# Last 64 value channels of a window-attention block: five products become three, with one more VectorE transpose and a GpSimd sum

## What is computed

```python
xl = roll(layernorm(transpose(x)), (-3, -3))                  # tokens x 192 channels
xw = windows(xl, 7)                                           # 49 tokens in each window
q, k, v = split(einsum('bnc,oc->bno', xw, qkv_w) + qkv_b)     # 6 heads of 32 channels
attn = softmax(einsum('bhnd,bmhd->bhnm', q, k) * 32 ** -0.5)
out = einsum('bhnm,bmhd->bnhd', attn, v)
out = out @ proj_w.T + proj_b
xl = layernorm(roll(unwindow(out), (3, 3)))
h = gelu(xl @ fc1_w.T + fc1_b) @ fc2_w.T + fc2_b              # 192 -> 768 -> 192
return transpose(h) + x
```

## Time and profile before

| | us |
|---|---|
| median of 3 runs | 2952.38 (2946.92 to 2953.0) |
| the profiled execution, whole | 2930.57 |
| its span in the trace | 2928.8 |
| TensorE busy | 2876.8 (98% of the span) |
| ScalarE busy | 2686.3 (92%) |
| VectorE busy | 2612.4 (89%) |
| GpSimd busy | 1287.7 (44%) |

### The profile page before, as it was taken

How to read it: one execution, slowest core, us unless ns; L and a number is a source line. 1 busy time by engine, 2 the same in 40 slices (tenths; PEclk the granted TensorE clock), 3 DMA queues, 4 the chain that set the end, 5 groups by cost and what they waited for, 6 DMA issues and landing times.

```text
span 2928.8 us, 72487 instructions
## 1 busy us (share of the span) xinstructions
PE 2876.8 (98%) x25004; PEld 2787.5 (95%) x25004; DVE 2612.4 (89%) x7211; ACT 2686.3 (92%) x5500; POOL 1287.7 (44%) x1549
## 2 busy tenths in 40 slices
PE   5999999999999999999999999999999999999998
PEld 4899999999999999999999999999999999999998
DVE  7889999999999999998989898999989999899985
ACT  2899999999999999999999999999999999999996
POOL 3444444444444444444444444444444444444432
PEclk9999999999999999999999999999999999999999
DMA  5344444434443444343444434444443443444431
GB/s 112 81 97 90 89 90 89 99 86 93 95 89 86 94 99 86 85 100 85 92 93 89 97 84 94 95 89 91 92 96 86 94 97 86 94 88 96 87 80 34
DMA packets 675019, 263.32 MB, mean 90 GB/s; under 512 B 505699, under 2 KB 633444, under 8 KB 674660
## 3 DMA queue, kind: packets, MB, share of 16 engines
q1 hardware_dynamic: 670724, 257.00, 40.9%
q10 hardware_dynamic: 3936, 1.68, 0.3%
HBM read 169.23 MB, written 89.27 MB: 88 GB/s over the span
## 4 chain that ended last, share of the span: by engine, by line
PE 81%; SPq 14%; DVE 1%; issue 1%; POOL 1%; DMA 1%; ACT 0%; POOLq 0%; DVEq 0%; ACTq 0%
PE psum L331 8%; PE psum L334 7%; PE psum L332 7%; PE psum L333 7%; PE psum L335 7%; PE psum L623 6%; PE psum L597 5%; PE psum L577 4%; PE psum L578 4%; PE psum L588 4%; PE psum L589 4%; PE psum L579 4%; PE psum L603 4%; SPq L410 3%; SPq L467 3%; PE psum L598 2%
## 5 line engine op out<-in xcount | busy, mean ns | idle before, releaser
L1268 POOL TENSOR_TENSOR pr<-pr,rc 98x294 f32<-98x294 f32 x512 | 384.5, 760 | 371.0 <-DVE rc L1079 371.0
L778 ACT ACTIVATE hh<-psum,b 128x392 fp32r<-128x392 f32 x768 | 451.3, 588 | 32.7 <-PE psum L589 6.4
L781 ACT ACTIVATE hf<-psum,b 128x392 f32<-128x392 f32 x768 | 451.3, 588 | 6.4
L1043 DVE TENSOR_TENSOR hl<-hf,hh 128x392 fp32r<-128x392 f32 x640 | 373.8, 599 | 4.2 <-ACT hf L781 4.1
L1241 POOL TENSOR_TENSOR ve<-mv,eps 104x4 f32<-104x4 f32 (+1 forms) x256 | 81.7, 319 | 660.0 <-DVE mv L1003 660.0
L1066 DVE TENSOR_REDUCE mx<-psum 98x6 f32<-98x294 f32 x512 | 229.1, 447 | 113.8 <-PE psum L598 113.5
L1262 POOL TENSOR_TENSOR hl<-hf,hh 128x392 fp32r<-128x392 f32 x128 | 133.2, 1041 | 358.7 <-ACT hf L781 358.7
L577 PE MATMUL psum<-hh,w2h 128*128 128x392 f32 x768 | 272.4, 355 | 0.0
L735 ACT ACTIVATE pt<-psum 113x294 f32<-113x294 f32 x512 | 205.8, 402 | 68.8 <-PE psum L603 68.6
L597 PE MATMUL psum<-km,qm 128*98 128x98 f32 x2048 | 260.8, 249 | 7.9 <-DVE xn L1008 3.9
L331 PE MATMUL psum<-x_h,w_mh 128*128 128x392 f32 x768 | 265.0, 345 | 0.7 <-DVE pr L1071 0.7
(11 more groups left out here) (135 smaller groups left out, 9929.0 us busy)
## 6 DMA issues: line engine op xcount, KB each, us to landing
bc<-mean_rstd SPq DMA_DIRECT2D x128, 392.0 KB, 3.7
xg<-in_x SPq DMA_DIRECT2D x368, 96.0 KB, 2.4
values_by_token<-vt_m SPq DMA_DIRECT2D x128, 256.0 KB
vbd<-values_by_token SPq DMA_DIRECT2D x256, 96.0 KB
xt<-in_x SPq DMA_DIRECT2D x112, 194.5 KB, 2.8
out<-xt SPq DMA_DIRECT2D x112, 194.5 KB, 3.3
values_by_token<-vt_r SPq DMA_DIRECT2D x128, 128.0 KB
vbd<-values_by_token SPq DMA_DIRECT2D x256, 51.0 KB
```

What stands on the lines that cost most here:

```text
L778: nc.scalar.activation(hh[:, m % HB, :], bank("fc1", m)[:, 0:T], ACT.Gelu, bias=b1[:, m:m + 1]).then_inc(s_hh, 1)
L781: nc.scalar.activation(hf[:, m % HB, :], bank("fc1", m)[:, 0:T], ACT.Gelu, bias=b1[:, m:m + 1]).then_inc(s_gelu, 1)
L1268: nc.gpsimd.tensor_tensor(probs(j), probs(j), each, ALU.mult).then_inc(s_prob, 1)
```

## The change

The high and the low weights of the last 64 value channels are laid side by side as one stationary tile of 128 columns, `wv_m` for the first 128 input channels and `wv_r` for the last 64. One matmul then gives the product with the high weights in PSUM partitions 0 to 63 and that with the low weights in 64 to 127. `values_rest` takes three matmuls in place of five. VectorE transposes the lower partial result (partitions 64 to 127) with one more instruction into a new tile `vt_l` in partitions 0 to 63, and GpSimd adds `vt_l` to `vt_r`. SyncE's queue waits for that sum before it writes `vt_r` to DRAM.

```diff
@@ last_read
             if name == "vt":
-                return s_vt, v, 2, i
+                return s_vt, v, 3, i + 1
@@ values_to_dram
-                sp.wait_ge(s_vt, nth(u, 2, 1))
+                sp.wait_ge(s_vt, nth(u, 3, 2))
...
                 sp.dma_start(by_token[u % 2, 0:CM], vt_m[:, u % 2]).then_inc(s_vd, 16)
+                sp.wait_ge(s_vsum, nth(u, 1, 0))
                 sp.dma_start(by_token[u % 2, CM:C], vt_r[:, u % 2]).then_inc(s_vd, 16)
@@ values_rest
-                claim(u, [("vt", 0)], (s_lo["x1"], 2, 1))
-                five(bank("vt", 0)[0:CR, 0:T], wq, CM, CR, [p[:, :] for p in x1]).then_inc(s_pe["vt"], 1)
+                claim(u, [("vt", 0)], (s_lo["x1"], 2, 0))
+                ps = bank("vt", 0)[:, 0:T]
+                nc.tensor.matmul(ps, wv_m[:, :], x1[0][:, :], start=True, stop=False)
+                nc.tensor.matmul(ps, wv_m[:, :], x1[1][:, :], start=False, stop=False)
+                pe.wait_ge(s_lo["x1"], nth(u, 2, 1))
+                nc.tensor.matmul(ps, wv_r[:, :], x1[2][:, :], start=False, stop=True).then_inc(s_pe["vt"], 1)
@@ split (once, before the loop)
+                if n == 0:
+                    for pair, raw_, of in ((wv_m, sm_, w[0]), (wv_r, sr_, w[2])):
+                        nc.vector.tensor_copy(pair[:, 0:CR], of[:, CM:C].bitcast(F32))
+                        nc.vector.tensor_tensor(pair[:, CR:128], raw_[:, CM:C], of[:, CM:C].bitcast(F32), ALU.subtract)
@@ v_out
-                blocks = bass.AP(psum, BANK_OF["vt", c] * 512, [[8 * 512, (CR, CM)[c]], [N, NW], [N - DH, 2], [1, DH]])
-                nc.vector.transpose((vt_r, vt_m)[c][:, u % 2], blocks).then_inc(s_vt, 1)
+                def blocks(r0, m):
+                    return bass.AP(psum, r0 * 8 * 512 + BANK_OF["vt", c] * 512, [[8 * 512, m], [N, NW], [N - DH, 2], [1, DH]])
+
+                if c == 0:
+                    nc.vector.transpose(vt_r[:, u % 2], blocks(0, CR)).then_inc(s_vt, 1)
+                    if u > 0:
+
+                        dve.wait_ge(s_vsum, nth(u - 1, 1, 0))
+                    nc.vector.transpose(vt_l[:, :, :, :], blocks(CR, CR)).then_inc(s_vt, 1)
+                else:
+                    nc.vector.transpose(vt_m[:, u % 2], blocks(0, CM)).then_inc(s_vt, 1)
@@ gpsimd
+            def last_values(u):
+
+                pool.wait_ge(s_vt, nth(u, 3, 1))
+                nc.gpsimd.tensor_tensor(vt_r[:, u % 2], vt_r[:, u % 2], vt_l[:, :, :, :], ALU.add).then_inc(s_vsum, 1)
@@ gpsimd step, after times_rstd_rest
+                if u[2] is not None:
+                    last_values(u[2])
```

More of the change, by code:

```diff
@@ L136, in swin_block_program @@
         w1 = [sb(f"w1_{p}", [128, NF], F32R) for p in ("mh", "ml", "rh", "rl")]
+        wv_m = sb("wv_m", [128, 128], F32R)
+        wv_r = sb("wv_r", [128, 128], F32R)
         w2h = sb("w2h", [128, MT, C], F32R)
@@ L188, in swin_block_program @@
         vt_r = sb("vt_r", [CR, 2, NW, 2, DH])
+        vt_l = sb("vt_l", [CR, NW, 2, DH])
         by_token = nc.dram_tensor("values_by_token", [2, C, NW, 2, DH], F32)
@@ L242, in swin_block_program @@
         s_vt = sem("values_by_token")
+        s_vsum = sem("last_values_summed")
         s_vd = sem("values_in_dram")
```

## The result

The changed kernel takes 2979.47 us (median of 4 runs, 2975.81 to 2980.7), the kernel before 2950.23 us beside it; the ratio is 1.0102, 95% interval 1.0083 to 1.0121. It is slower by 1.0%, 29 us, where 23 us were forecast; its profiled execution took 2978.32 us. A second comparison, beside the experiments, gave 1.0130 (1.0114 to 1.0145). The kernel before took 2950 us in the first comparison and 2928 to 2931 us in the four rounds of the experiments, which ran on three chips; the chip of the first comparison is not known, so it is not shown that a chip makes this difference.

A forecast was written before the change was run, and what follows sets the result against it. The prediction took TensorE as the bound, busy 2746 of 2750 us. A longer step (20 us) plus GpSimd's sum (3 us) made 23 us slower, from 2952.38 to 2975 us (+0.8%), range 2946 to 2994.

The forecast's parts named there:

- The slack of 0.21 us at `project`: Time from the end of VectorE's `vt_m` to TensorE's weight load for `project` 0, taken as the deciding number.
- Two matmuls at 0.18 us each: TensorE in `values_rest`: two products fewer free 0.36 us a step, 45 us over 124 steps.
- so I take nothing for it: TensorE in `values_rest`: 128 output columns in place of 64 cost the remaining three products nothing.
- The transpose: VectorE ahead of `o_r`: one more transpose adds 0.63 to 0.71 us a step, 0.71 taken.
- Release and reload: TensorE at `project`: starts 0.06 or 0.14 us after `vt_m` ends, then loses 0.05 to 0.10 us reloading weights.
- I take the middle, 0.16: Growth of one step, stated as 0.05 to 0.26 us; over 124 steps, middle 20 us slower.
- the cheap transpose: VectorE's new transpose by plain overlap with its neighbour: 0.63 us in place of 0.71.
- The sum on GpSimd: Before `rstd`: about 1.4 us long, mostly covered by idle time; costs 0 to 8 us in all, 3 taken.
- SyncE's queue: Stores and loads behind the new wait for the sum: delay hidden or already priced, nothing taken.
- the work before the loop: Four small VectorE instructions building the paired weights, hidden by a 6.2 us DMA wait; nothing taken.
- Rival A: TensorE keeps its gain of 0.36 us a step: 45 us faster, 2907 us; chance 0.17.
- Rival C: GpSimd's sum contends with VectorE, grows to some 2.5 us, delays `xn` in half the steps: 3006 us; chance 0.06.

The follow-up runs named there:

- the late transpose: The changed kernel with VectorE's transpose of the lower partial result moved behind `vt_m`; ratio 1.0008 to the kernel before.
- three matmuls alone: The changed kernel without `vt_l`, its transpose and GpSimd's sum; ratio 0.9958 to the kernel before.
- late transpose and swap: The changed kernel with the lower transpose behind `vt_m` and ScalarE's `gelu_full` of tile 1 ahead of the first `k_rest_out`; ratio 0.9978 to the kernel before.

## Why the prediction was right

*The slack of 0.21 us at `project`* decided, as said: 124 waits there, none elsewhere of any size. Shown by the late transpose, which takes this wait away and leaves the work of every engine as it is. Of the 0.21 us the release itself takes 0.11; the prediction has it as a term of its own.

*Two matmuls at 0.18 us each.* Right as the price of two products more of the same kind (0.34 us a step with five against three). But the step "so I take nothing for it", on the 128 columns, left out the first weight load: the change frees 0.30 us of TensorE, not 0.36. It did not matter for the forecast, since I let VectorE use only 0.30; from the row maximum to `xt` it is now 8.15 us (1518.08 to 1526.23) against 8.43, so 0.28.

*The transpose.* Forecast 0.71 us in a range from 0.63. It took 0.72 us, and its follower starts 0.76 us after it started (1527.57 to 1528.33); from `xt` to the end of `vt_m` it is 3.72 us against 2.97, so 0.75. The new transpose and its follower each start only after the one before has ended (1527.55 to 1527.57, 1528.29 to 1528.33), as the rule that the prediction quotes from the Trainium skill (VectorE: DVE Perf Modes, section "Two Vector instructions with no wait between them") has it.

*Release and reload.* Forecast 0.06 to 0.14 and 0.05 to 0.10 us. Measured 0.11 from the end of `vt_m` to the load and 0.14 to the product; the second product of `project` then comes 0.14 us after the first (1530.09 to 1530.23), where it was 0.08 (1525.38 to 1525.46), so reloading costs 0.06. With these the step closes: from the start of the row maximum to the end of `vt_m` 11.87 us in place of 11.40, from there to `project` 0.14 in place of 0.39, and from `project` to the next row maximum 10.51 in place of 10.48, together 0.25.

*The term that was too small* is "I take the middle, 0.16" for the growth of the step: 0.26 was measured, the upper end of the stated 0.05 to 0.26. With 0.71 as chosen for the transpose the working gives 0.13 to 0.26; the middle that I took also weighed the cheap transpose, which I had already set aside. This is 12 us of the sum.

*The sum on GpSimd.* Forecast 1.4 us long, 0 to 8 us in price, 3 taken; 1.35 us long and about 7 us in price. The median needs no further term: 32 + 7 = 39 us is above the 29 us of the first comparison and beside the 38 us of the second (0.0130 x 2931). Why the two comparisons differ by 0.3% was not tried. That the 29 us lie so near to the forecast 23 is therefore in part luck: the mechanism was right, but its terms as measured give 39.

*SyncE's queue and the work before the loop* cost nothing that was seen: the queue waited for the sum twice, 2.2 us. The four small instructions ended before VectorE's wait for the DMA, which was 7.0 us (6.2 before).

*Rival A was priced wrongly*, though it was rejected for the right reason. "TensorE keeps its gain" was to give 45 us. No more than 0.30 x 124 = 37 us were there to gain, and three matmuls alone, where nothing is added on VectorE, gave 0.42%, 12 us. I had looked for waits of TensorE and found none, but not for waits with almost no slack on other engines: ScalarE's `hf` 1 had 0.16 us.

*Rival C*, contention of GpSimd with VectorE, is real, in regular steps too: it stretches `ym` in a quarter of the steps, where the prediction had half with a delay of `xn`. `xn` waits for GpSimd 1.9 us in all (200 to 2850 us), the idle time at the row maximum takes up most of the rest, and its price is within the 7 us of the sum.

## What to carry to other kernels

Where one engine is busy all the time and three others run close behind, an edit is priced by the slack of each semaphore wait around it, in the timeline of one step, not by occupancy: 0.7 us of VectorE ahead of a releasing instruction cost 0.41 us a step more (22.53 us) than behind it (22.12). A wait further on that is idle anyway, such as that at the row maximum, takes up what is stretched ahead of it. Look for the second smallest slack too, for it bounds what the first repair can bring. A wait shorter than the overlap of two products does not show as idle time of TensorE; only the distances of the starts tell.

## What was not expected of the hardware

Operations with two SBUF inputs on VectorE and operations on GpSimd at the same time can stretch to about twice their length, now on one engine, now on the other, now on both (`hl` 1.0 to 2.1 us a pair, GpSimd's product 1.05 to 2.20 us, `ym` 0.55 to 0.99 us beside a sum that kept its 1.28). In the execution with late transpose and swap, steps over the regular length, up to 26.2 us long, added 27 us, where they added 5 in the kernel before. The same kernel took 0.7% longer in the first comparison than in the later rounds, which agreed within 0.12% over three chips.
